# The video expert's late columns first in a mixture's products: a change to the order of matmuls in a four-layer kernel

## What is computed

```python
vm = expert_mask(token_type_ids)[..., None]       # which tokens go to the video expert
residual = hidden_states
x = rms_norm(hidden_states, ln_in_w)
mixed = jnp.where(vm, x @ v_qkv, x @ l_qkv)       # queries, keys, values
q, k, v = jnp.split(mixed, 3, axis=-1)
...
ctx = sdpa(q, k, v, causal=True)
attn_out = jnp.where(vm, ctx @ v_dense, ctx @ l_dense)
hidden_states = residual + attn_out
...
```

## Time and profile before

| | us |
|---|---|
| median of 3 runs | 1384.76 |
| lowest and highest of them | 1384.41, 1391.71 |
| the profiled execution's own time | 1382.84 |
| its span, first to last instruction | 1380.9 |
| between span and time of that execution | 1.9 |

### The profile page before, as it was taken

The page is one execution under the profiler, slowest core; times in us unless marked ns, Lnnn a source line. Parts: engine busy times, 40 slices in busy tenths (PEclk is TensorE's granted clock), DMA queues, the critical chain, the costliest instruction groups (busy, mean ns, idle before and its releaser), DMA issues.

```text
span 1380.9 us, 25903 instructions
## 1 busy us (share of the span) xinstructions
PE 1306.9 (95%) x10931; PEld 1047.3 (76%) x10931; DVE 764.5 (55%) x1361; ACT 473.6 (34%) x785; POOL 452.1 (33%) x559
## 2 busy tenths in 40 slices
PE   7978899999999998999999999998899999999988
PEld 5755677787887776888888888876678777787767
DVE  4455576666666656354354444446667566666543
ACT  3323333423324222244445543433332333323321
POOL 1143444444344342311111111324434344334332
PEclk9978999999999999999999999999999999999999
DMA  9010000000001001110000000011000000000000
GB/s 324 8 61 1 2 2 2 1 2 2 2 2 47 2 5 48 50 60 1 0 1 1 1 0 1 1 42 42 1 2 1 9 9 2 1 17 2 1 16 17
DMA packets 19901, 27.29 MB, mean 20 GB/s; under 512 B 3432, under 2 KB 15552, under 8 KB 19520
## 3 DMA queue, kind: packets, MB, share of 16 engines
q1 hardware_dynamic: 19008, 24.20, 5.2%
q10 hardware_dynamic: 768, 1.26, 0.3%
HBM read 23.35 MB, written 2.10 MB: 18 GB/s over the span
## 4 chain that ended last, share of the span: by engine, by line
PE 84%; DVE 6%; ACT 5%; POOL 3%; issue 2%; ACTq 0%; DVEq 0%; POOLq 0%
PE bank L1433 6%; PE bank L1723 6%; PE bank L1688 5%; PE bank L1693 5%; PE bank L1577 5%; PE bank L1933 4%; PE bank L1940 4%; PE bank L1897 4%; PE row_banks L1527 4%; PE row_banks L1837 3%; PE row_banks L1560 3%; PE bank L1495 3%; PE bank L1712 3%; PE bank L1426 3%; PE row_banks L1532 2%; ACT room L2051 2%
## 5 line engine op out<-in xcount | busy, mean ns | idle before, releaser
L1283 POOL TENSOR_SCALAR_AFFINE_SELECT room<-room 128x1024 f32<-128x1024 f32 x64 | 70.7, 1107 | 185.3 <-ACT room L2051 185.3
L2293 DVE TENSOR_REDUCE room<-row_banks 128x4 f32<-128x512 f32 (+1 forms) x128 | 116.4, 952 | 23.1 <-PE row_banks L1532 22.8
L2051 ACT ACTIVATE room<-row_banks 128x1536 f32<-128x1536 f32 x64 | 92.9, 1451 | 90.0 <-PE row_banks L1560 90.0
L1723 PE MATMUL bank<-room,down_w 128*128 128x256 f32 x384 | 95.9, 391 | 0.5 <-DVE room L2393 0.5
L2307 DVE RECIPROCAL room<-bank 128x256 f32<-128x256 f32 x32 | 56.1, 1754 | 59.3 <-PE bank L1577 59.3
L2083 ACT ACTIVATE room<-bank 128x256 f32<-128x256 f32 x96 | 36.4, 383 | 148.6 <-PE bank L1693 137.6
L1245 POOL TENSOR_TENSOR room<-room 128x256 f32<-128x256 f32 x32 | 24.5, 767 | 173.0 <-ACT room L2063 173.0
L1723 PEld LDWEIGHTS bank<-room,down_w 128*128 128x128 f32 x384 | 70.4, 192 | 14.0 <-issue 4.9
L1357 POOL TENSOR_TENSOR room<-room 128x512 f32<-128x512 f32 x32 | 33.7, 1070 | 133.1 <-DVE room L2495 132.9
L1560 PE MATMUL row_banks<-room 32*128 32x256 f32 (+1 forms) x1024 | 62.1, 357 | 9.7 <-ACT room L2051 4.6
L1560 PEld LDWEIGHTS row_banks<-room 32*128 32x128 f32 x1024 | 48.9, 190 | 27.6 <-issue 15.6
(11 more groups left out here) (243 smaller groups left out, 3022.4 us busy)
## 6 DMA issues: line engine op xcount, KB each, us to landing
out_x<-wq SPq DMA_DIRECT2D x8, 256.0 KB, 2.4
qkv<-in_L_xattn_v_qkv SPq DMA_DIRECT2D x2, 768.0 KB, 5.6
qkv<-in_L_xattn_l_qkv SPq DMA_DIRECT2D x2, 768.0 KB, 8.6
gate_w<-in_L_xattn_v_gate SPq DMA_DIRECT2D x2, 640.0 KB, 8.0
gate_w<-in_L_xattn_l_gate SPq DMA_DIRECT2D x2, 640.0 KB, 7.4
up_w<-in_L_xattn_v_up SPq DMA_DIRECT2D x2, 640.0 KB, 6.1
up_w<-in_L_xattn_l_up SPq DMA_DIRECT2D x2, 640.0 KB, 6.4
down_w<-in_L_xattn_v_down SPq DMA_DIRECT2D x2, 640.0 KB, 6.0
```

The costliest lines, as they stand in the source:

```text
L1283: pool.affine_select(out=diagonal, in_=diagonal, compare_op=ALU.is_ge, fill=0.0, base=0, pattern=[[0, 8], [1, P]], channel_multiplier=-1)\
L1723: return pe.matmul(ff_bank[0][:, t * S:(t + 1) * S], down_w[:, f, t * P:(t + 1) * P], hid[:, i, :], start=(i == t == 0), stop=(i == UPS - ...
L2051: act.activation(probs[w % 2], row_banks[:, :, 0:3 * P], ACT.Exp).then_inc(*ATT_ACT.does(e, f"exp{w}"))
L2293: last = dve.tensor_reduce(dst, row_banks[:, :, P * i:P + S * i], X, ALU.max, negate=True)
```

## The change

`to_experts` puts the video expert first: the 64 late columns with start=True, then the branch and its part, and only then the wait for y_l and the four matmuls of the other expert. The wait for y_l (or ctx_l) moves from the callers into the function, behind the video part; the first wait is now the one for y_v (or ctx_v).

```diff
-                def to_experts(e, out, w, at, y_l, y_v, v_ready):
+                def to_experts(e, out, w, at, y_l, l_ready, y_v, v_ready):
 
-                    def first_expert(lo, hi, stop):
+                    def first_expert(lo, hi, start):
                         for t in range(KT):
                             for k in range(KT):
-                                last = pe.matmul(out[:, t * S + lo:t * S + hi],
+                                pe.matmul(out[:, t * S + lo:t * S + hi],
                                           w[:, 0, k, at + t * P:at + (t + 1) * P], y_v[:, k, lo:hi],
-                                                 start=False, stop=(stop and k == KT - 1), skip_group_check=True)
-                        return last
+                                          start=(start and t == k == 0), stop=False, skip_group_check=True)
 
+                    pe.wait_ge(*v_ready)
+                    first_expert(LATE, S, True)
+                    with pe.If(has_early[e % B]):
+                        first_expert(0, LATE, False)
+                    pe.wait_ge(*l_ready)
                     for t in range(KT):
                         for k in range(KT):
-                            pe.matmul(out[:, t * S:(t + 1) * S], w[:, 1, k, at + t * P:at + (t + 1) * P],
-                                      y_l[:, k, :], start=(t == k == 0), stop=False, skip_group_check=True)
-                    pe.wait_ge(*v_ready)
-                    with pe.If(has_early[e % B]):
-                        first_expert(0, LATE, False)
-                    return first_expert(LATE, S, True)
+                            last = pe.matmul(out[:, t * S:(t + 1) * S], w[:, 1, k, at + t * P:at + (t + 1) * P],
+                                             y_l[:, k, :], start=False, stop=(k == KT - 1), skip_group_check=True)
+                    return last
...
-                    pe.wait_ge(*N0_DVE.did(e, "yl"))
-                    to_experts(e, ff_bank[1], qkv, 0, n0_yl, n0_yv, N0_DVE.did(e, "yv")).then_inc(*QKV_PE.does(e, "q"))
+                    to_experts(e, ff_bank[1], qkv, 0, n0_yl, N0_DVE.did(e, "yl"), n0_yv, N0_DVE.did(e, "yv")).then_inc(*QKV_PE.does(e, "q"))
...
-                    pe.wait_ge(*ATT_POOL.did(e, "cl"))
-                    to_experts(e, crs_bank, dense, 0, ctx_l, ctx_v, ATT_POOL.did(e, "cv")).then_inc(*CRS_PE.does(e, "dense"))
+                    to_experts(e, crs_bank, dense, 0, ctx_l, ATT_POOL.did(e, "cl"), ctx_v, ATT_POOL.did(e, "cv")).then_inc(*CRS_PE.does(e, "dense"))
```

More of the change, by code:

```diff
@@ L1419, in trig @@
                     last.then_inc(*X_PE.does(e, "trig"))
-                def to_experts(e, out, w, at, y_l, y_v, v_ready):
-                    def first_expert(lo, hi, stop):
+                def to_experts(e, out, w, at, y_l, l_ready, y_v, v_ready):
+                    def first_expert(lo, hi, start):
                         for t in range(KT):
                             for k in range(KT):
-                                last = pe.matmul(out[:, t * S + lo:t * S + hi],
-                                                 w[:, 0, k, at + t * P:at + (t + 1) * P], y_v[:, k, lo:hi],
-                                                 start=False, stop=(stop and k == KT - 1), skip_group_check=True)
-                        return last
+                                pe.matmul(out[:, t * S + lo:t * S + hi],
+                                          w[:, 0, k, at + t * P:at + (t + 1) * P], y_v[:, k, lo:hi],
+                                          start=(start and t == k == 0), stop=False, skip_group_check=True)
[4 more added lines that the diff above has]
+                    pe.wait_ge(*l_ready)
                     for t in range(KT):
                         for k in range(KT):
-                            pe.matmul(out[:, t * S:(t + 1) * S], w[:, 1, k, at + t * P:at + (t + 1) * P],
-                                      y_l[:, k, :], start=(t == k == 0), stop=False, skip_group_check=True)
-                    pe.wait_ge(*v_ready)
-                    with pe.If(has_early[e % B]):
-                        first_expert(0, LATE, False)
-                    return first_expert(LATE, S, True)
+                            last = pe.matmul(out[:, t * S:(t + 1) * S], w[:, 1, k, at + t * P:at + (t + 1) * P],
+                                             y_l[:, k, :], start=False, stop=(k == KT - 1), skip_group_check=True)
+                    return last
                 def sum_squares(sq, out):
@@ L1488, in k @@
                         pe.wait_ge(*B_ACT.did(e - 2, "gelu3"))
-                    to_experts(e, ff_bank[0], qkv, D, n0_yl, n0_yv, N0_DVE.did(e, "yv")).then_inc(*QKV_PE.does(e, "k"))
+                    to_experts(e, ff_bank[0], qkv, D, n0_yl, N0_DVE.did(e, "yl"), n0_yv, N0_DVE.did(e, "yv")).then_inc(*QKV_PE.does(e, "k"))
                 def v(e):
```

## The result

| | before | after |
|---|---|---|
| median of 13 runs each, us | 1384.41 | 1393.10 |
| lowest and highest, us | 1383.31, 1392.04 | 1389.99, 1394.29 |
| the profiled execution's own time, us | 1382.84 | 1390.64 |
| its span, us | 1380.9 | 1388.7 |
| its mean granted clock of PE | 0.981 | 0.976 |

The ratio of after to before is 1.0062, with a 95% interval of 1.0052 to 1.0071. The change makes the kernel slower by 0.6%, 8.7 us between the medians; the profiled executions differ by 7.8 us in span. The prediction was 1385.6 us, in a range from 1383.2 to 1388.0. It was wrong.

A forecast was written before the change was run, and what follows sets the result against it. The prediction took PE, busy 95% of the span, to bound the kernel. Its four parts summed 0 + 0 + 0.85 + 0 = +0.85 us, so 1384.76 + 0.85 = 1385.6 us, range 1383.2 to 1388.0.

The forecast's parts named there:

- The bound: Whole kernel: PE bounds it, busy 95% of the span and 84% of the chain that ended last.
- Part 1: q and k products starting on y_v: gain 0, since eight flag reads, not y_l, bound the first q.
- Part 2: Dense products: moving the wait for ctx_l gains 0, since PE waits there for the emptied bank.
- Part 3: Matmul order on PE: 17 calls followed by 32-row tile groups pay 0.05 us more each, +0.85 us.
- Part 4: Branch, now behind 0.84 us of matmuls instead of 1.73: its 0.205 us stays covered, cost 0.
- the sum: Whole kernel: 0 + 0 + 0.85 + 0 = +0.85 us, added to the median of 1384.76 for 1385.6.
- rival (d): Elsewhere in the kernel: small shifts of some tenths of a us move waits by up to 2 us; 1383 to 1388, chance 0.07.
- rival (b): First q: short matmuls come first and the clock's rise fails, +1.6 us, 1387.2; chance 0.08.
- slower: Whole kernel slower by more than 0.5%, 6.9 us, by an exposed branch or a little of rival (d); chance 0.04.

The follow-up runs named there:

- the reads moved: Changed kernel with each flag read during the first stage of its sample, instead of eight in a row ahead of the first q: 1392.18 us, ratio 1.005.
- The filled pair: Kernel before and changed kernel, each with overwritten matmuls (90 records) in PE's idle times behind which the clock fell: 1377.40 us (old order), 1378.34 us (new order).
- Filling only the first place: Changed kernel with three overwritten matmuls in PE's idle time ahead of the dense product of sample 7: 1388.98 us, ratio 1.0047.
- more filling: Old-order kernel of the filled pair, with five and three more overwritten matmuls in idle times of sample 1's attention: 1377.80 us, ratio 0.996.

## Why the prediction was wrong

**The bound** was read rightly: PE is the bound, at 95%. But what PE's time is made of was read only as records and idle time, not as records at one clock or the other.

**Part 1 held.** In the changed kernel the sequencer and then all engines at the first q:

```profile
L1471 PEldq TENSOR_LOAD <-early x8: 295/304/497, 83.1 to 85.8; - x8
...
84.71 0.69 DVE L2246 TENSOR_TENSOR room<-room,is_vis 128x512 f32<-128x512 f32 x1
85.43 0.69 DVE L2248 TENSOR_TENSOR room<-room 128x512 f32<-128x512 f32 x1
86.31 1.94 PE L1426 MATMUL bank<-room,qkv 128*128 128x64 f32 x8 [2.55 <-DVE room L2248]
```

y_v is there at 85.40 and PE starts at 86.31, behind the last read (85.8 + 0.3 = 86.1), as in the earlier trace rows. The kernel with the reads moved shows that they bound it. One argument was weak, though: 0.18 us from release to start was called too long for DVE's release. With the reads gone it was still 87.36 - 87.21 = 0.15 us at half clock. The row that carried the argument was the reads' end, not the lag.

**Part 2 held.** The timeline of PE in the changed kernel at the dense product of sample 7:

```profile
505.67 1.17 PE L1426 MATMUL bank<-room,dense 128*128 128x64 f32 x8 [1.69 <-DVE room L2321]
506.62 3.61 PE L1437 MATMUL bank<-room,dense 128*128 128x256 f32 x8
510.07 0.59 PE L1687 MATMUL bank<-room,gate_w 128*128 128x256 f32 x2
```

1.69 us of waiting for the emptied bank, as in the earlier trace rows. But the same rows show what the prediction had no term for: 510.07 - 506.62 = 3.45 us for eight records that take 1.78 elsewhere. This one group loses 1.67 us to the clock, twice the whole sum of the prediction.

**Part 3 held.** The timeline of PE in the changed kernel, near 109 us with a tiled group behind the product and near 148 us with none:

```profile
107.31 1.00 PE L1426 MATMUL bank<-room,qkv 128*128 128x64 f32 x8
108.15 1.95 PE L1437 MATMUL bank<-room,qkv 128*128 128x256 f32 x8
110.03 0.94 PE L1527 MATMUL row_banks<-room 32*128 32x128 f32 x16
...
146.15 1.00 PE L1426 MATMUL bank<-room,qkv 128*128 128x64 f32 x8
146.98 1.95 PE L1437 MATMUL bank<-room,qkv 128*128 128x256 f32 x8
148.76 1.46 PE L1495 MATMUL bank<-qkv,room 128*128 128x256 f32 x6
```

1.78 us (148.76 - 146.98) inside, 1.88 to a following L1527 (110.03 - 108.15), and 2.72 for the call where the earlier trace rows give 2.66. The sum can be read too: from 104 to 505 us, where a tiled group follows 8 times, after loses 1.10 - 0.71 = 0.39 us on before, 0.05 a time; 17 times make the 0.85. The filled pair has 0.94 us for the whole.

One reading behind this part was wrong, without harm to its price. The prediction divided 0.54 us by 16 and took a load of L1527 for 0.034 us, against 0.105 for a short product's spacing. Taken singly, these 32-row loads last 0.181 to 0.187 us each, and the 128-row loads of L1426 beside them 0.190 to 0.192; the 32-row ones start four at a time, 0.007 us apart, one such four every 0.11 us. So these rows do not speak against a load's time going by its columns. The 0.05 and 0.09 us were read from starts and stand without it; why a tiled group costs 0.09 more is open.

**Part 4 held.** L1437 has no idle time ahead of it in 384 records (the groups above), so the branch stays covered. The branches of the changed kernel:

```profile
L1432 PEldq COMPARE_BRANCH  x48: 200/205/355, 86.3 to 1325.5; - x48
```

**The step that failed** is in the sum and in rival (d): "small shifts of some tenths of a us move waits elsewhere by up to 2 us either way". Every price was worked out at full clock and added to a time whose clock was taken as given. The clock was weighed at one place, the first q (rival (b)), where it did rise, at 90.1 us. It was not weighed at the other idle times, though the table of stretches behind the earlier trace rows, asked for the whole span, would have shown half clock at 900, 961, 995 and 1343 us, behind idle times of PE of 2.25 and 1.03, 1.17 and 1.34, 0.84 and 1.03, and 2.34 us. The kernel before had such an idle time at 505 us as well, 1.69 us ahead of the dense product of sample 7, behind which its clock stayed up. A shift by 0.2 us or the new order at that one place was enough to change that, and the 0.4 us that part 3 had rightly put on PE by then is such a shift. The missing term is about 8 us: 8.7 between the medians less the 0.85 of part 3, and likewise 8.9 less 0.85 in the profiled executions from the first product on. And the 0.04 given to "slower" was too little: one of the three runs shown for before lay at 1391.71 us, which says that this kernel can move by 7 us with no edit at all (two of its 13 runs did, though none of the 69 beside the experiments).

The Trainium skill, TensorE: Matmul & The Clock Gate, section "Part 1: The HAM clock gate (the "warmup" mystery)", calls the cost of the ramp less than 1% of a typical kernel's span, and tells the modeller not to fit a particular count of slow matmuls. The page speaks of a ramp. In these traces the clock isn't at half at the start alone but at 507, 900 and 1000 us too, 51 us in the kernel before. What the change added to that, about 8 us, is under 1% of the span as well, 0.6%, but it is nearly all of the change's effect.

**What stays open.** Shown: the order of the matmuls, not the wait, carries the loss; a fall at 507 us comes from the order at that place alone as well as from a mere shift; PE's work in the idle time prevents it; and the price of the order at full clock is 0.05 us for each call with a tiled follower, read up to 505 us. Not shown: why a short group behind an idle time lets the clock fall where a long one at the same position doesn't; and what makes the later stretches longer (902-909, 964-971 and 1001-1012 us against 900-904, 962-965 and 996-1003). Filling only the first place gave back some 4 us of 8.7, so the later ones depend on the position at which the kernel comes to them, or on the order there; that wasn't taken apart. Single runs differ too: those of after go from 1389.99 us at a mean clock of 0.979 to 1394.20 at 0.972.

## What to carry to other kernels

Before an edit of a PE-bound kernel is priced, list all the stretches in which the granted clock is at half and all the idle times of PE ahead of them. Here the falls stood behind idle times of 0.8 to 2.5 us, though not behind all of that size: before had 1.65 us at 133, 1.50 at 528 and 1.48 at 1317 us with no fall behind them. A shift of such places by 0.2 us, from one added matmul, cost 4.6 us in all. Where such idle times can't be removed, try matmuls in them whose result is overwritten: here that gave 6 us. It didn't always make the times steady: the four runs with the old order lie within 0.2 us, the ten with the new one within 4.9, and the ten with more filling within 11.2. To learn what an edit costs by itself, read the distances between starts where the clock is at full in both traces, and compare it with and without in kernels so filled, since in the bare one the clock covers the answer.

## What the runs showed of the hardware

- The same idle time of PE (1.69 us, busy 1.41 of 3.10 us) at the same distance from the last rise of the clock (336.63 and 336.65 us) was followed by full clock with long matmuls behind it and by half clock with short ones; and by half clock with the long ones too, 0.2 us later.
- A matmul of 0.43 us added at 262 us cost 4.6 us; six of them cost 4.4 us.
- Sixteen weight loads of 32x128 last 0.18 us each and take 0.54 us together, since four start at a time; one of 128x128 lasts 0.19 us.
- 90 added records in PE's idle time (half of a matmul each, 0.43 / 2 us, so 19 us of streaming) made the kernel 6 us faster.
- At half clock the lag from DVE's release to PE's start was 0.15 us (at 87 us with the reads moved), against 0.06 us at full (at 506 us in before); each was read once.
